# Values of key blocks 1 to 3 in one run of TensorE work, and the value projection two batch rows ahead

## The chip, the cores and the metric

One NeuronCore of one Trainium2 chip runs the whole program. The metric is device time in microseconds (us) of one launch, from three runs. TensorE is called PE in the profile (PEld is its weight load), VectorE DVE, ScalarE ACT, GpSimd POOL, and SyncE SP, which only issues DMAs here.

## The reference

The input is 8 batch rows of 512 tokens with 128 channels. Three stages of work alternate with mixture-of-experts layers:

- a first attention, 16 heads of 8 channels, whose keys and values are halved in length by a convolution (512 queries against 256 keys, no mask);
- a second attention, causal, 512 against 512, with its own layer norm;
- a third and a fourth attention, causal, run together as one stage of 16 batch rows.

Per head, `att = softmax(q k^T / sqrt(8))` (masked above the diagonal where it is causal) and `out = att v`, followed by an output projection and a residual sum.

## The kernel before

`attention` (L511) works in units. A unit is one batch row b and one group g of 4 heads, so a batch row has 4 units (u = 4b + g), and a causal stage has 32 or 64 units. In each causal unit PE goes through 12 slots. Slot i computes a score chunk of unit u (L781, keys on the partitions, then mask matmuls L648) and a "max" tile of unit u+2 (L665, queries on the partitions, then mask matmuls L648). ACT exponentiates each chunk out of PSUM into `pt` (L858), and DVE reduces each max tile to `mx` (L1008). Score chunks rotate over `RING = 3` PSUM banks and max tiles over three others, so slot i may start only when ACT has read chunk i-3 and DVE has read tile i-3 (`score_wait`, `max_wait`, `before`). Slots 0 to 3 are 512 columns wide, 4 to 7 are 384, 8 and 9 are two heads of 256, and 10 and 11 two heads of 128.

Everything else that PE does is put between slots by `order(u)`: for each name the dictionary `when` gives the slot behind which it stands. Each engine's program is written out from the same order, so a copy on ACT or DVE stands at the same place in its queue.

- `value_p` and `value0`, `value1` are the matmuls of `pt` with the values (`values`, L725). For one key block kb they are 8 instructions, 32 columns of the array each, four side by side. `early` says which key blocks are done in the unit itself, and `late` which are done in the next unit under the name `value_p`.
- `max_T` is a transpose of `mx` (L680). Its result goes by ACT (`nm`, L890), four POOL operations (L1161 to L1167) and three DMAs (L1290, `put_max`) into row 52 and the next two of `qa`. Slot 0 of the next unit waits for their landing (`m_landed`).
- `o_T`, `ctx_T`, `out` (L737, L744, L751) transpose and project the attention's result. `x_T`, `q`, `k`, `v` (L689, L695, L702, L707) prepare a later batch row. All of these, and `max_T`, use PSUM bank `MISC` one after another (`take_misc`), and each is copied out by ACT (x_T, q, k, ctx_T, nm) or DVE (o_T, out, v).
- `value_rows` (L998) copies v from PSUM to the buffer `vst`, and `spread` on POOL (L1150) takes it from there to `vs`, one group of heads a unit.
- `f_moments`, `f_T`, `f_l` prepare the next mixture layer's routing; `moments` are layer-norm moments for batch rows to come (L149, L152).

Of the kernel before, what the change touches and what calls it, by code (L numbers as in the profile page):

```python
# [25 lines left out]
P = 128  # L26
# [7 lines left out]
B, S, C = 8, 512, 128  # L34
T = B * S
NT = T // P
TB = S // P
H, D = 16, 8
# [472 lines left out]
def attention(nc, k, segments, r):  # L511
# [17 lines left out]
    LATE_ROOT = {3: 3, 7: 4, 11: 5}  # L529
    LAST = len(r.phases) - 1  # L530
    SENT_IN = {-6: (0, 1), -5: (1, 4), -4: (4, 5), -3: (5, 8), -2: (8, 12), -1: (12, 16)}
    entered = lambda b: sum(first <= b for first, n in ENTRY_GROUPS)

    if causal:
        chunks = ([(0, (h,), 512) for h in (0, 1, 2, 3)] + [(1, (h,), 384) for h in (0, 1, 2, 3)]
                  + [(kb, heads, S - kb * P) for kb in (2, 3) for heads in ((0, 2), (1, 3))])
        maxes = ([(3, (h,), 512) for h in (1, 0, 3, 2)] + [(2, (h,), 384) for h in (1, 0, 3, 2)]
                 + [(qb, heads, (qb + 1) * P) for qb in (1, 0) for heads in ((1, 3), (0, 2))])
        when = {"value_p": 2, "max_T": 2, "o_out": 2, "nm": 2, "o_T": 5, "value0": 8, "x_T": 8, "k": 5, "ctx_T": 8,
                "q": 11, "v": 11, "out": 5, "value1": 11, "moments": 4, "f_moments": 4, "f_T": 8, "f_l": 11,  # L540
                "late0": 0, "late2": 6, "late_root": 0, "choose": 6, "ranks": 5, "mark": 6, "f_rows": 0,
                "choose0": 8, "ranks0": 8, "find0": 9, "choose1": 7, "choose2": 9, "choose3": 1, "ranks1": 9,
                "find1": 10, "choose4": 1}
        last_front = (11, 8, 11, 3, 8, 11)
        early, late = ((0,), (1,)), (2, 3)
    else:
        chunks = [(kb, (h,), 512) for kb in range(KB) for h in (0, 1, 2, 3)]
        maxes = [(qb, heads, nk) for qb in range(TB) for heads in ((1, 3), (0, 2))]
        when = {"value_p": 2, "max_T": 2, "o_out": 2, "nm": 2, "o_T": 4, "x_T": 5, "k": 5, "ctx_T": 5, "value0": 6,
                "q": 7, "v": 7, "out": 7, "moments": 3, "f_moments": 3, "f_T": 5, "f_l": 7,  # L550
                "late0": 0, "late2": 4, "late_root": 0, "choose": 5, "ranks": 4, "mark": 5, "f_rows": 0}
        last_front = (7, 5, 7, 3, 6, 7)
        early, late = ((0,),), (1,)
# [10 lines left out]
    def order(u):  # L564
# [6 lines left out]
            events += [("o_out", u // 2 - 1), ("o_T", u // 2 - 1)]  # L571
        if u + 1 < U:
            events += [("max_T", u + 1), ("nm", u + 1)]
        if g == 0 and b + 1 < NB:
            events += [("v", b + 1)]
        if u in LATE_ENTRY:
            events += [("late0", LATE_ENTRY[u])]
        if u - 1 in LATE_ENTRY and u:
# [7 lines left out]
        if u == U - 2:  # L586
            events += [("f_rows", b - 1)]
        if g == 3 and FIRST + 3 <= b < NB - 1:
            events += [("f_T", b - 3), ("f_l", b - 3)]
        fronts = []  # L590
        if b == NB - 1 and g < 3:
            names = (("f_T", 4),), (("f_l", 4), ("f_T", 5)), (("f_l", 5), ("f_T", 6), ("f_l", 6))
# [41 lines left out]
    with nc.Block() as block:  # L634
# [3 lines left out]
        def _(pe):  # L638
# [168 lines left out]
            for t in range(NMX):  # L807
                max_tile(1, t)
                if t in (2, 5):
                    project(ENTRY[t // 3], 1)  # L810
            project("k", 1)
            for u in range(U):
                for name, n in order(u):
                    if name == "score":
                        slot(u, n)
                    elif name == "max_T":
                        max_transpose(n)
                    elif name == "value_p":
                        for kb in late:
                            values(n, kb)  # L820
                    elif name[:-1] == "value":
                        for kb in early[int(name[-1])]:
                            values(n, kb)
                    elif name in ("x_T", "q", "k", "v"):
                        project(name, n)
                    elif name in ("o_T", "ctx_T", "out", "f_T", "f_l"):
                        tail(name, n)
                    elif name in ("ranks0", "ranks1"):
                        take_misc()
                        ranks(pe, k, r, n)  # L830
                        misc[0] = (s.ranks_read, n + 1)
                    elif name == "ranks":
                        ranks(pe, k, r, n)
# [91 lines left out]
        def _(dve):  # L925
# [67 lines left out]

            def value_rows(b):
                dve.wait_ge(*s.v_full.at(b + 1))
                if b >= 1:
                    dve.wait_ge(*s.vs_ready.at(4 * b))
                nc.vector.tensor_copy(k.vst[:, 0:KB, :], PS[:, MISC, 0:KB * P].rearrange("p (t c) -> p t c", c=P))\  # L998
                    .then_inc(s.v_free.h, 1)

            def max_tile(u, t):
# [52 lines left out]
            for t in range(NMX):  # L1054
                max_tile(1, t)
                if t == 5 and conv:
                    convolve(1)
            entry(2, 2)
            entry_deviations(2)
            for u in range(U):  # L1060
                for name, n in order(u):
# [6 lines left out]
                    elif name in ("o_T", "out"):  # L1068
                        tail(name, n)
                    elif name == "late2":  # L1070
                        entry(2, n)
                    elif name == "late_root":
                        entry_deviations(n)
                    elif name == "moments":
                        later_moments(n)
                    elif name == "f_moments":
                        front_moments(n).then_inc(s.fm_ready.h, 1)
                    elif name == "f_rows":
                        front(n)
                    elif name == "choose0":  # L1080
                        if n == 0:
                            dve.wait_ge(*s.gl_free.at(r.phases[0][1] // TB))
                        choose(nc, k, route, r, 0, (n,))
                    elif name in ("choose1", "choose2", "choose3"):
                        if n == 0:
                            dve.wait_ge(*s.gl_free.at(r.phases[1][1] // TB))
                        choose(nc, k, route, r, 1, (n,))
                    elif name in ("find0", "find1"):
                        find_ranks(nc, k, route, r, n)
                    elif name in ("choose", "choose4"):  # L1090
                        dve.wait_ge(*s.gl_free.at(r.phases[n][1] // TB))
                        choose(nc, k, route, r, n)
                    elif name == "mark":
                        find_ranks(nc, k, route, r, n)
                        dve.wait_ge(*s.pv_done.at(U - 1))
                        mark_tiles(nc, k, route, r, 0)
# [28 lines left out]
        def _(pool):  # L1125
# [18 lines left out]
            def spread(b, g):  # L1144
                if g == 0:
                    pool.wait_ge(*s.v_free.at(b + 1))
                if b >= 1:
                    pool.wait_ge(*s.pv_done.at(4 * b - 3 + g))
                pair, n = g // 2, g % 2
                pool.tensor_copy(k.vs[:, g, 0:KB, :, n * D:(n + 1) * D], k.vst[:, 0:KB, pair * 64:pair * 64 + 64]  # L1150
                                 .rearrange("p t (h n d) -> p t h n d", h=HG, n=2)[:, :, :, n, :]).then_inc(s.vs_ready.h, 1)

            def max_split(u):
# [510 lines left out]
def program(nc, a, out):  # L1664
    ctx = ExitStack()
    with ctx:
# [39 lines left out]
        k.work = sb("work", [4, S])  # L1706
        k.q32, k.k32, k.rest, k.restk = (k.work[:, i, :] for i in range(4))
        k.parts = sb("parts", [2, 3, S], BF16)
        k.vst = sb("vst", [TB, C])
        k.vs = sb("vs", [G, TB, HG, 32])  # L1710
        k.qa, k.ka = sb("qa", [2, G, 2, S], BF16), sb("ka", [2, G, 2, S], BF16)
        k.mx = sb("mx", [2, 16])
# [325 lines left out]
```

## Time and profile before

| | us |
|---|---|
| median of 3 runs | 1950.85 (1948.93 to 1954.16) |
| the profiled execution's own time | 1948.95 |
| its span in the trace | 1947.2 |
| PE busy | 1548.6 (80%) |
| DVE busy | 1297.8 (67%) |
| POOL busy | 1078.7 (55%) |
| ACT busy | 966.4 (50%) |

The span is the time from the first to the last instruction; 1.75 us of the execution lie around it. A row of the timeline gives an instruction's or a run's start, its length, engine, line, operation and what it writes and reads, and in brackets how long the engine sat idle before it and what released it. Of matmuls that overlap, the length of a run is that of their union.

### The profile page before, as it was taken

How to read it: one execution, taken by the hardware profiler on the slowest of the kernel's cores; microseconds unless marked ns; L12 is line 12 of the kernel's file. 1: busy time of each engine (PE TensorE's matmuls, PEld its weight loads, DVE VectorE, ACT ScalarE, POOL GpSimd, SP SyncE). 2: the span in 40 equal slices, each digit the busy share in tenths (PEclk: the TensorE clock that was granted, in tenths of full speed). 3: DMA queues.
4: the chain of work that ended last, by engine and by line, in shares of the span. 5: the costliest groups of instructions: out<-in, count | busy, mean ns of one | idle time of the engine just before them, and what ended most of it. 6: DMA issues, size and time to landing. Idle time of an engine off the chain costs nothing. (4 is left out here: it accounts for less than half of the span.)

```text
span 1947.2 us, 46256 instructions
## 1 busy us (share of the span) xinstructions
PE 1548.6 (80%) x17646; PEld 941.7 (48%) x17646; DVE 1297.8 (67%) x3322; ACT 966.4 (50%) x2039; POOL 1078.7 (55%) x1712
## 2 busy tenths in 40 slices
PE   5648788876599999854798599999999999744993
PEld 4532333345255555433576355555555555423772
DVE  7348888782688878734421688888888887544324
ACT  4215667732166677520233166777777776411331
POOL 3447766505378775545355376555757765552552
PEclk9977999977599999865799599999999999755996
DMA  8443322204333223100343442332323322001445
GB/s 288 112 131 104 90 82 80 75 23 123 114 120 104 82 88 99 42 28 23 114 138 98 138 126 84 92 100 78 113 84 98 97 81 83 26 23 56 141 130 156
DMA packets 233185, 188.08 MB, mean 97 GB/s; under 512 B 30044, under 2 KB 221368, under 8 KB 232326
## 3 DMA queue, kind: packets, MB, share of 16 engines
q1 hardware_dynamic: 222582, 166.36, 28.5%
q0 software_dynamic: 10240, 18.76, 2.9%
q8 instruction: 141, 2.31, 0.5%
q14 instruction: 78, 0.64, 0.1%
q10 hardware_dynamic: 144, 0.00, 0.0%
HBM read 104.34 MB, written 80.74 MB: 95 GB/s over the span
## 5 line engine op out<-in xcount | busy, mean ns | idle before, releaser
L1008 DVE TENSOR_REDUCE mx<-PS 128x2 f32<-128x512 f32 (+3 forms) x1408 | 784.2, 612 | 189.0 <-PE PS L648 137.5
L858 ACT ACTIVATE pt<-PS 128x512 f32<-128x512 f32 (+2 forms) x1408 | 667.6, 537 | 312.1 <-PE PS L648 227.6
L665 PE MATMUL PS<-ka,qa 52*128 52x256 bf16 (+3 forms) x2048 | 461.7, 305 | 65.2 <-DVE mx L1008 47.4
L781 PE MATMUL PS<-qa,ka 55*128 55x512 bf16 (+3 forms) x1792 | 459.7, 321 | 41.3 <-DMA qa<-nm 17.8
L725 PE MATMUL PS<-pt,vs 128*32 128x512 f32 (+3 forms) x3584 | 349.6, 481 | 2.3 <-issue 1.5
L648 PE MATMUL PS<-mask_q,identh 64*128 64x64 bf16 x3072 | 299.5, 193 | 1.5 <-issue 1.4
L648 PE MATMUL PS<-mask_k,identh 64*128 64x64 bf16 x3072 | 299.0, 192 | 0.9 <-issue 0.9
L781 PEld LDWEIGHTS PS<-qa,ka 55*128 55x128 bf16 x1792 | 166.9, 94 | 273.7 <-issue 119.3
L648 PEld LDWEIGHTS PS<-mask_k,identh 64*128 64x128 bf16 x3072 | 249.2, 97 | 51.7 <-issue 6.8
L648 PEld LDWEIGHTS PS<-mask_q,identh 64*128 64x128 bf16 x3072 | 252.4, 98 | 31.0 <-issue 8.9
L1161 POOL CAST nm<-nm 16x128 bf16<-16x128 f32 x128 | 36.2, 283 | 340.1 <-ACT nm L890 329.3
L665 PEld LDWEIGHTS PS<-ka,qa 52*128 52x128 bf16 x2048 | 172.1, 95 | 97.9 <-DVE mx L1008 63.3
L415 POOL DMA_INDIRECT xe_rows<-xn,slot x128 | 128.4, 1003 | 93.2 <-DVE slot L402 56.2
L1398 PE MATMUL PS<-pt 128*128 128x128 f32 x1280 | 155.7, 280 | 9.4 <-ACT pt L1422 6.3
L1422 ACT ACTIVATE pt<-PS,f1b 128x512 f32<-128x512 f32 x128 | 87.6, 687 | 152.2 <-PE PS L1386 148.9
L1386 PE MATMUL PS<-pt 128*128 128x512 f32 (+1 forms) x384 | 155.6, 551 | 4.5 <-issue 2.6
L1398 PEld LDWEIGHTS PS<-pt 128*128 128x128 f32 x1280 | 151.0, 196 | 11.8 <-issue 11.6
L1524 POOL DMA_INDIRECT y_rows<-pt,idx x80 | 79.4, 992 | 113.5 <-DVE pt L1489 95.2
L725 PEld LDWEIGHTS PS<-pt,vs 128*32 128x32 f32 x3584 | 82.2, 110 | 75.7 <-issue 27.3
L1386 PEld LDWEIGHTS PS<-pt 128*128 128x128 f32 x384 | 74.4, 204 | 58.8 <-issue 52.4
L1479 DVE TENSOR_SCALAR pt<-PS,l2w,l2b 128x512 f32<-128x512 f32 x32 | 25.9, 810 | 98.1 <-PE PS L1376 93.2
L1516 POOL DMA_INDIRECT pt<-xn_rows,idx x32 | 31.3, 977 | 98.1 <-issue 56.5
(249 smaller groups left out, 2333.4 us busy)
## 6 DMA issues: line engine op xcount, KB each, us to landing
pt<-in_f_w SPq DMA_DIRECT2D x96, 256.0 KB
qa<-q_parts SPq DMA_DIRECT2D x256, 96.0 KB, 2.3
ka<-k_parts SPq DMA_DIRECT2D x192, 96.0 KB, 2.3
q_parts<-parts SPq DMA_DIRECT2D x32, 384.0 KB, 3.4
k_parts<-parts SPq DMA_DIRECT2D x24, 384.0 KB, 2.6
xn<-y_rows SPq DMA_DIRECT2D x32, 256.0 KB, 3.2
hid<-y_rows SPq DMA_DIRECT2D x32, 256.0 KB, 3.7
q_parts<-parts SPq DMA_DIRECT2D x32, 256.0 KB, 3.2
```

The source lines that it names most:

```text
L415: pool.indirect_dma_start(k.xe_rows[:, :], bass.IndirectOffsetOnAxis(k.slot[:, c, t:t + 1], 0), k.xn[:, t * P:(t + 1) * P], None, bounds_c ...
L648: mm = pe.matmul(PS[:, bank, col + j * HALF:col + (j + 1) * HALF], k.identh[half * HALF:(half + 1) * HALF, j, :], table[half * HALF:(half ...
L665: mm = pe.matmul(PS[:, bank, i * n:(i + 1) * n], k.qa[rows, b % 2, g, h // 2, qb * P:(qb + 1) * P], k.ka[rows, b % 2, g, h // 2, 0:n], sta ...
L725: mm = pe.matmul(PS[32 * h:32 * h + 32, O_BANK, q0:S], k.vs[:, g, kb, h, :], k.pt[:, u % 2, at[c] + i * n:at[c] + (i + 1) * n], start=(kb ...
L781: mm = pe.matmul(PS[:, bank, i * n:(i + 1) * n], k.ka[rows, b % 2, g, h // 2, kb * P:(kb + 1) * P], k.qa[rows, b % 2, g, h // 2, q0:S], st ...
L858: nc.scalar.activation(k.pt[:, u % 2, at[c]:at[c] + len(heads) * n], PS[:, SC_BANK + c % RING, 0:len(heads) * n], ACT.Exp, scale=SCORE_SCA ...
L1008: nc.vector.tensor_reduce(out, PS[:, MX_BANK + t % RING, 0:len(heads) * n] .rearrange("p (h n) -> p h n", n=n), AX.X, ALU.max).then_inc(s. ...
L1161: pool.tensor_copy(hi, full).then_inc(s.nm_hi.h, 1)
L1386: pe.matmul(PS[:, H_BANK + f, 0:capacity], k.w1[:, par, f * P:(f + 1) * P], k.xeT[:, par, 0:capacity], start=True, stop=True).then_inc(s.h ...
L1398: mm = pe.matmul(PS[:, Y_BANK + par, t * P:(t + 1) * P], k.hT[:, par, f, t * P:(t + 1) * P], k.w2[:, par, f, :], start=(f == 0 and t == 0) ...
L1422: nc.scalar.activation(k.hT[:, e % 2, f, 0:capacity], PS[:, H_BANK + f, 0:capacity], GELU, bias=w.b1[:, e * FC + f:e * FC + f + 1]).then_i ...
L1524: pool.indirect_dma_start(k.y_rows[:, :], bass.IndirectOffsetOnAxis(k.idx[:, 1, n:n + 1], 0), k.ys[e % RING_E][:, t, :], None).then_inc(s. ...
```

## The change

In the causal stages the four places between slots (behind 2, 5, 8 and 11) become three (behind 3, 7 and 11), with `value_p` now holding key blocks 1, 2 and 3 in place of 2 and 3, and key block 0 behind slot 7. `x_T` and `ctx_T` move from behind slot 8 to behind slot 11, `q` stays there. The value projection `v` of batch row b+1, done in group 0 of b, becomes that of b+2, done in group 3 of b; so a second buffer for its rows is needed (`vst_other`, which lies over the convolution's `cv`; in the first attention the two halves of `vst` serve), and v of row 1 is done before the first unit. In the first attention `k`, `f_T`, `f_l` and `v` move too. `f_l` now stands in group 0 of the following batch row. DVE gets a wait for its own end behind `f_moments`.

```diff
+    vst = lambda b: (k.vst, k.vst_other)[b % 2] if causal else k.vst[:, b % 2 * KB:(b % 2 + 1) * KB, :]
     if causal:
-        when = {"value_p": 2, "max_T": 2, "o_out": 2, "nm": 2, "o_T": 5, "value0": 8, "x_T": 8, "k": 5, "ctx_T": 8,
-                "q": 11, "v": 11, "out": 5, "value1": 11, "moments": 4, "f_moments": 4, "f_T": 8, "f_l": 11,
+        when = {"value_p": 3, "max_T": 3, "o_out": 3, "nm": 3, "o_T": 7, "value0": 7, "x_T": 11, "k": 7, "ctx_T": 11,
+                "q": 11, "v": 11, "out": 7, "moments": 4, "f_moments": 4, "f_T": 9, "f_l": 5,
...
-        last_front = (11, 8, 11, 3, 8, 11)
-        early, late = ((0,), (1,)), (2, 3)
+        last_front = (9, 8, 11, 5, 9, 11)
+        early, late = ((0,),), (1, 2, 3)
     else:
-        when = {"value_p": 2, "max_T": 2, "o_out": 2, "nm": 2, "o_T": 4, "x_T": 5, "k": 5, "ctx_T": 5, "value0": 6,
-                "q": 7, "v": 7, "out": 7, "moments": 3, "f_moments": 3, "f_T": 5, "f_l": 7,
+        when = {"value_p": 2, "max_T": 2, "o_out": 2, "nm": 2, "o_T": 4, "x_T": 5, "k": 4, "ctx_T": 5, "value0": 6,
+                "q": 7, "v": 7, "out": 7, "moments": 3, "f_moments": 3, "f_T": 6, "f_l": 3,
...
-        if g == 0 and b + 1 < NB:
-            events += [("v", b + 1)]
+        if g == 3 and b + 2 < NB:
+            events += [("v", b + 2)]
...
         if g == 3 and FIRST + 3 <= b < NB - 1:
-            events += [("f_T", b - 3), ("f_l", b - 3)]
+            events += [("f_T", b - 3)]
+        if g == 0 and FIRST + 4 <= b:
+            events += [("f_l", b - 4)]
...
             project("k", 1)
+            project("v", 1)
...
             def value_rows(b):
                 dve.wait_ge(*s.v_full.at(b + 1))
-                if b >= 1:
-                    dve.wait_ge(*s.vs_ready.at(4 * b))
-                nc.vector.tensor_copy(k.vst[:, 0:KB, :], ...
+                if b >= 2:
+                    dve.wait_ge(*s.vs_ready.at(4 * (b - 1)))
+                nc.vector.tensor_copy(vst(b)[:, 0:KB, :], ...
...
+            value_rows(1)
             entry(2, 2)
...
                         front_moments(n).then_inc(s.fm_ready.h, 1)
+                        dve.wait_ge(*s.fm_ready.at(n - FIRST + 1))
...
-        k.vst = sb("vst", [TB, C])
+        k.vst, k.vst_other = sb("vst", [TB, C]), k.cv[:, :, :].rearrange("p j (t c) -> p (j t) c", c=C)
```

## Rows read from the trace of the kernel before

**Rows 1.** Busy time by window: stretch, its length, engines' busy time, PEclk, DMA share, GB/s.
```profile
155.20:410.00 254.80, 213.36 (x1582) 89.62 (x1581) 215.82 (x469) 170.96 (x341) 162.10 (x317) 0.95 0.28 84
1115.20:1667.30 552.10, 524.17 (x8437) 305.13 (x8436) 464.65 (x1037) 396.91 (x889) 352.35 (x638) 0.99 0.31 93
```

**Rows 2.** The same view for single units: four of one batch row, then a fifth.
```profile
1331.29:1340.61 9.32, 9.02 (x150) 5.70 (x146) 8.00 (x16) 6.54 (x15) 8.81 (x14) 1.00 0.45 153
1340.61:1348.71 8.10, 8.10 (x145) 4.94 (x142) 6.75 (x14) 6.37 (x14) 4.86 (x9) 1.00 0.40 110
1348.71:1357.29 8.58, 8.58 (x139) 4.76 (x135) 7.24 (x15) 6.52 (x15) 1.63 (x5) 1.00 0.19 52
1357.29:1365.92 8.63, 7.81 (x135) 4.05 (x132) 7.40 (x20) 6.40 (x15) 5.73 (x10) 1.00 0.22 60
...
1124.23:1132.12 7.89, 7.69 (x137) 4.45 (x134) 6.16 (x13) 6.30 (x14) 7.24 (x12) 1.00 0.35 93
```

**Rows 3.** Timeline of PE in the unit at 1340.61: its four pieces.
```profile
1341.55 0.86 PE L725 MATMUL PS<-pt,vs 128*32 128x256 f32 x16
1342.34 0.28 PE L680 MATMUL PS<-ident,mx 128*16 128x128 f32 x1
...
1343.41 1.16 PE L751 MATMUL PS<-a1wo,ctxT 128*128 128x128 f32 x8
...
1345.45 0.63 PE L689 MATMUL PS<-ident,xa 128*128 128x128 f32 x4
1346.00 1.07 PE L725 MATMUL PS<-pt,vs 128*32 128x512 f32 x8
...
1347.81 0.19 PE L648 MATMUL PS<-mask_q,identh 64*128 64x64 bf16 x1
1347.93 0.85 PE L725 MATMUL PS<-pt,vs 128*32 128x384 f32 x8
```

**Rows 4.** Timeline of PE, the pieces that only other units of the row have.
```profile
1336.25 0.63 PE L744 MATMUL PS<-ident,ctx 128*128 128x128 f32 x4 [0.30 <-DVE ctx L1020]
...
1338.73 1.16 PE L707 MATMUL PS<-a1wv,xnT 128*128 128x128 f32 x8
...
1351.52 0.66 PE L737 MATMUL PS<-ident,osb 128*128 128x128 f32 x4
...
1355.45 1.13 PE L695 MATMUL PS<-xnT,afwq 128*128 128x512 f32 x2
```

**Rows 5.** Groups by shape, 1331.29 to 1365.92: count, then busy us, mean ns, idle before.
```profile
L1008 DVE TENSOR_REDUCE mx<-PS 128x1 f32<-128x512 f32 x16 | 10.3, 686 | 2.8 <-PE PS L648 2.6
L1008 DVE TENSOR_REDUCE mx<-PS 128x1 f32<-128x384 f32 x16 | 8.1, 549 | 0.0
```

**Rows 6.** Timeline of DVE in the unit at 1340.61, then of ACT around 1357.29.
```profile
1341.14 3.56 DVE L1008 TENSOR_REDUCE mx<-PS 128x1 f32<-128x512 f32 x6 [0.52 <-PE PS L648]
...
1356.62 0.69 ACT L880 ACTIVATE work<-PS,afqb 128x512 f32<-128x512 f32 x1 [0.61 <-PE PS L695]
1357.78 1.58 ACT L858 ACTIVATE pt<-PS 128x512 f32<-128x512 f32 x3 [0.47 <-PE PS L648]
```

**Rows 7.** Timeline of PE, slots 3 to 8 of the unit at 1124.23.
```profile
1126.17 0.39 PE L781 MATMUL PS<-qa,ka 55*128 55x512 bf16 x1
...
...
1127.31 0.33 PE L781 MATMUL PS<-qa,ka 55*128 55x384 bf16 x1 [0.20 <-ACT pt L858]
1127.46 0.33 PE L665 MATMUL PS<-ka,qa 52*128 52x384 bf16 x1
...
1128.15 0.27 PE L781 MATMUL PS<-qa,ka 55*128 55x256 bf16 x1
```

**Rows 8.** Timeline, the three DMAs of `put_max` in two units, and one wait for them.
```profile
221.69 1.59 SPq L1290 DMA_DIRECT2D qa<-nm  x3
...
224.40 0.39 PE L781 MATMUL PS<-qa,ka 55*128 55x512 bf16 x1 [1.63 <-DMA qa<-nm]
...
1344.64 1.59 SPq L1290 DMA_DIRECT2D qa<-nm  x3
```

More of the change, by code:

```diff
@@ L995, in value_rows @@
                 dve.wait_ge(*s.v_full.at(b + 1))
-                if b >= 1:
-                    dve.wait_ge(*s.vs_ready.at(4 * b))
-                nc.vector.tensor_copy(k.vst[:, 0:KB, :], PS[:, MISC, 0:KB * P].rearrange("p (t c) -> p t c", c=P))\
+                if b >= 2:
+                    dve.wait_ge(*s.vs_ready.at(4 * (b - 1)))
+                nc.vector.tensor_copy(vst(b)[:, 0:KB, :], PS[:, MISC, 0:KB * P].rearrange("p (t c) -> p t c", c=P))\
                     .then_inc(s.v_free.h, 1)
@@ L1149, in spread @@
                 pair, n = g // 2, g % 2
-                pool.tensor_copy(k.vs[:, g, 0:KB, :, n * D:(n + 1) * D], k.vst[:, 0:KB, pair * 64:pair * 64 + 64]
+                pool.tensor_copy(k.vs[:, g, 0:KB, :, n * D:(n + 1) * D], vst(b)[:, 0:KB, pair * 64:pair * 64 + 64]
                                  .rearrange("p t (h n d) -> p t h n d", h=HG, n=2)[:, :, :, n, :]).then_inc(s.vs_ready.h, 1)
```

## The prediction

> **What bounds the kernel now.** I read the busy time by window first, because the share over the whole span mixes stages. In the long causal stage PE is busy 524 of 552 us at a granted clock of 0.99 [rows 1]; DVE has 465 and ACT 397. The first attention is another case: PE 213 of 255 us, DVE 216, neither full [rows 1]. Then I took single units. Three of the four units of a batch row have PE busy for all or nearly all of 9.32, 8.10 and 8.58 us; the fourth idles 0.8 us of 8.63 (it holds the DVE work `moments`) [rows 2]. A row takes 34.63 us. So PE's order of work sets the pace there, and DVE (6.75 to 8.00 us a unit) is close behind. That second fact matters, since PE and DVE can only overlap by as much as three PSUM banks hold.
>
> The timeline of PE shows what a unit is made of: slots, which run without a gap, and four pieces between them. A piece costs its own busy time and 0.05 us: from the last mask at 1347.81 to the next unit's start at 1348.71 are 0.90 us, for 0.85 of values [rows 2, 3].
>
> **The pieces now.** With that 0.05, in us: values 2 and 3 with `max_T` 0.86 + 0.28, overlapping, 1.12; `out` 1.21; `o_T` 0.71; `q`, and `k` of the same shape, 1.17; key block 0 alone 1.12, key block 1 alone 0.90; `x_T` (the shape of `ctx_T`, 0.63) and block 0 1.72; `ctx_T` and block 0 with a wait of 0.30 for DVE 2.04; `v` and block 1 1.99; `q` and block 1 1.96 [rows 3, 4]. The units of a row have pieces of 5.86, 4.95, 4.91 and 4.31, together 20.0. The second unit (8.10) has no idle time, so its twelve slots take 8.10 - 4.95 = 3.15, four times that is 12.6, and 34.63 - 12.6 - 20.0 = 2.0 us a row are waits between slots.
>
> **What the change saves.** How much of a piece is the break itself? Block 0 has 128 columns more than block 1 and takes 1.07 against 0.85, so 0.22 for 128 columns; 384 columns are then 0.66, and 0.24 of the 0.90 is the break [rows 3]. A row has 16 breaks now and 12 after: 4 x 0.24 = 0.96. The wait of `ctx_T` goes too, 0.30: `o_T` will stand behind slot 7 and `ctx_T` behind 11, and slot 11 can't start before DVE has read tile 8, which it does behind `o_T`'s division. Pieces after: 20.0 - 1.26 = 18.7 us a row. Moving `v` by one unit moves 1.16 us of PE [rows 4] and a DVE copy of 512 columns, 0.7 by the reduce of the same width [rows 5], and adds neither.
>
> **What it costs.** Now each piece comes after three slots, and three banks are what may be filled ahead. After it comes a fourth slot, whose bank DVE must have emptied. A unit starts at 1340.61 and DVE starts on tile 0 at 1341.14, 0.53 later [rows 2, 6]; the reduce takes 0.69 [rows 5]; to PE's next start I add 0.06, so that it is 1.28 (the 1.29 measured below has this distance in it). Three slots take 0.84, from 1340.61 to just before the values at 1341.55 less a lead of 0.12 [rows 2, 3]. Wait: 0.43. A slot of 384 columns is by estimate 0.05 shorter than the 0.28 of one of 512, and its tile there as much sooner: 0.48 + 0.55 + 0.06 = 1.09 against 0.70, wait 0.39. For slots 8 to 11 (the first two hold 512 columns again, the last 256) I take 0.41, the mean.
>
> The trace has one place with the same situation. The unit at 1124.23 has no piece behind slot 5. Its slot 3 starts at 1126.17, and slot 6 should start three slots, 0.28 + 0.23 + 0.23 = 0.74, later. Its score starts at 1127.31, released by ACT, and its max tile at 1127.46, 1.29 after slot 3: 0.55 late [rows 7]. And this unit, which lacks the `out` piece of 1.21 us, is only 0.21 shorter than the second one (7.89 against 8.10) [rows 2]. The breaks behind every third slot are time in which DVE and ACT catch up; PE pays for it anyway.
>
> There is one more loss. A copy on ACT stands in front of the next exponentials. Now every such piece but `out` and `o_T` has values behind it that hide the copy (`x_T`, `ctx_T`, `q`), and `k`'s falls between slots 5 and 6. After, `x_T`, `ctx_T` and `q` stand alone behind slot 11. The copy of q begins 0.11 after its matmuls end and takes 0.69, so the exponential of slot 0 starts at 0.80 instead of 0.49 (1357.78 - 1357.29) [rows 2, 6]. An exponential takes 0.60 (three, half a microsecond apart, end 1.58 after the first's start), so slot 3 waits until 0.80 + 0.60 + 0.06 = 1.46 instead of 0.84: 0.61 in place of 0.43. `v`'s copy on DVE does the same. The copy `o_out` in every second unit comes just before slot 4's exponential, but begins while PE still transposes; I add 0.09 there, 0.48 for 0.39.
>
> Waits after, for a row: slot 3 4 x 0.61 = 2.44, slot 7 2 x 0.39 + 2 x 0.48 = 1.74, slot 11 4 x 0.41 = 1.64: 5.8. The row's sum: 12.6 + 18.7 + 5.8 = 37.1 against 34.6. DVE's `moments` no longer count: they stand behind slot 4, and the tiles they delay are wanted only behind the piece after slot 7. That is inside the sum, since the 2.0 of old waits isn't carried over. So +2.5 us a batch row.
>
> The Trainium skill speaks against the change as well: Perfetto Trace Analysis, section Identifying Performance Opportunities, says that the same gap again and again on the engine that should be saturated can mean that SBUF or PSUM has no room for the next tile. By that rule PE would show one gap for each group of four slots; the trace so far agrees with it in the one unit above, with 0.55 us. The sum would be the same by it.
>
> **The sum.** There are 24 causal batch rows. The last of each stage is full of other waits, and I leave both out. Of the 22 left the six at b = 0 to 2 have late layer-norm work on DVE, and waits there that a break would have cost nothing; half the loss for them. 16 x 2.5 + 6 x 1.25 = 48. `v` of row 1 stands ahead of each causal stage, where PE comes from idling: its 1.16 us doubled if the clock is at its lower level there, and 1.16 given back in unit 0, so 1 a stage, 2 for both. Where the `f_` pieces stand alone they break a group of four, which gives back what their break costs; nothing. The first attention: PE and DVE both have 40 us to spare in 255, v and k move into unit 3 of a row; nothing, at most 3 us either way. DVE's added wait: 12 times some 0.1, beside other idle time.
>
> 1948.95 (span 1947.2 and 1.75 around it) + 48 + 2 = 1999 for an execution like the profiled one, whose time is 1.9 under the median of the runs. I take **2001 us**.
>
> **Bounds.** Below: if ACT's copies cost nothing, and only 0.43 + 0.39 + 0.41 of waits a unit stay, a row has 4.9 of waits, +1.6, and the sum is 1951 + 16 x 1.6 + 6 x 0.8 + 2 = 1983; with a break worth 0.1 more, 4 x 0.1 x 22 = 9 less, 1974. Above: the full loss in all 22 rows, 55, and waits of the measured 0.55 at slots 7 and 11 and 0.61 at slot 3, 6.8 a row in place of 5.8, another 22: 2030.
>
> **Rivals.**
>
> *The path of the maxima ends last.* `max_T` moves behind slot 3 and all of the values. It starts at 1.73 in a unit now; then at 1.46 + 0.28 + 0.12 + 0.66 (block 1) + 0.79 (blocks 2 and 3, 1341.55 to 1342.34) = 3.3. The DMAs start 2.30 after it (1344.64 - 1342.34) [rows 3, 8] and have landed 2.7 after their start, as where PE waited for them (221.69 to 224.40) [rows 8]: 8.3, in a unit of 9.3 on average: 1 us of slack, where the second unit now has 8.1 - 1.73 - 2.3 - 2.7 = 1.4. For: POOL and SP have other work queued ahead of it in the first and last unit of a row, and each may make it later. It decides from 1 us on. If it then ends last in every unit by half a microsecond, 22 x 2 = 44 more: 2045. 0.08.
>
> *PE gains.* The waits at the fourth slots lie under what PE's queue does meanwhile, or the banks are free sooner than I read. Then what counts is pieces and slots: 22 x 1.26 = 28 less, 1923, and if half the old waits go too, 1900. It decides at 1.26 us of new waits a row, so 0.1 at each of 12 fourth slots. For: 0.24 a break is real. Against: 0.55 was measured in one such slot [rows 7]. 0.08. The Trainium skill, same page, section Optimizing Tensor Performance, says that matmul groups should rotate through PSUM banks so that the reading of one overlaps the matmuls of the next. Both versions do rotate, and by this rule the reading is covered, which is this rival's 1923.
>
> *It cancels.* New waits of 12 x 0.27 = 3.3 us a row, beside no old ones: within 0.3% of before. Against: 0.27 is less than the reduce's 0.69 allows. 0.04.
>
> *The clock falls* in the causal stages, as PE idles more. The first attention has PE busy at 84% and a granted clock of 0.95 [rows 1]; the sum gives the causal ones about 31.3 of 37.1, 84% too. Going from 0.99 to 0.95 over the 552 us of the long stage and about half as much of the short one is 0.04 x 830 = 33, most of it hidden behind the new waits; a third of it, 11, gives 2012, inside the range. It is part of the chance of the main case, 0.80.
>
> So faster by over 0.3% 0.08, within 0.3% 0.04, slower by over 0.3% 0.88; 0.3% is about what a measurement of this kernel tells from no change. The range, 1968 to 2035, takes in the bounds of the main case and a few us for the start, the first attention and the clock on either side.
>
> **What would show it.** In the profile after: a causal unit of 9.0 to 9.6 us instead of 8.1 to 9.3; PE idle before L781 or L665 at slots 3, 7 and 11 with ACT `pt` L858 and DVE `mx` L1008 as releasers, some 0.4 to 0.7 each; 12 pieces in a row, of 18.7 us; the wait of `ctx_T` gone, `moments` without a wait. DVE and ACT idle in front of a unit's first tile for longer, about 1 us. The prediction fails if slot 3 doesn't wait, if the waits of `qa<-nm` come to tens of us, or if the row at 1331 to 1366 is under 34.6.

## The result, and the profile after

The changed kernel took 2028.26 us (median of 4 runs, 2021.62 to 2040.24), the kernel before in the same measurement 1950.67: a ratio of 1.040, 95% interval 1.035 to 1.044. The forecast was 2001 with a range to 2035, so the sign and the size came, 27 us short of the median. The profiled execution took 2026.74, its span is 2025.0 against 1947.2.

Where did 77.8 us go? The first view is the busy time by window, cut at the first score of each attention stage and at its end. Of the kernel before (stretch, length, busy PE, PEld, DVE, ACT, POOL, granted clock, DMA):

```profile
155.20:409.70 254.50, 213.06 (x1581) 89.52 (x1580) 215.56 (x467) 170.86 (x341) 162.10 (x317) 0.95 0.28 84
409.70:537.88 128.18, 76.02 (x516) 57.24 (x513) 72.88 (x264) 24.08 (x50) 47.84 (x54) 0.65 0.33 97
537.88:877.92 340.04, 295.50 (x4358) 170.19 (x4359) 256.07 (x628) 210.87 (x467) 221.70 (x370) 0.92 0.26 79
877.92:1115.16 237.24, 171.13 (x1028) 121.84 (x1024) 95.15 (x282) 54.47 (x83) 112.75 (x118) 0.77 0.34 101
1115.16:1725.73 610.57, 560.13 (x8773) 325.48 (x8774) 490.20 (x1117) 416.18 (x931) 377.40 (x668) 0.96 0.28 87
```

The same view of the changed kernel, and below it the four units of one steady batch row, which answer to [rows 2]:

```profile
155.91:415.47 259.56, 217.85 (x1577) 88.55 (x1577) 215.28 (x467) 170.46 (x340) 159.89 (x315) 0.94 0.27 81
415.47:546.72 131.25, 78.88 (x525) 59.72 (x521) 71.67 (x254) 25.09 (x51) 47.72 (x54) 0.65 0.35 102
546.72:908.45 361.73, 305.29 (x4351) 177.50 (x4351) 257.30 (x629) 210.64 (x467) 220.74 (x370) 0.90 0.23 72
908.45:1150.82 242.37, 170.61 (x1029) 122.35 (x1030) 94.77 (x281) 55.02 (x84) 112.39 (x118) 0.76 0.34 103
1150.82:1802.84 652.02, 580.81 (x8767) 339.83 (x8767) 492.79 (x1121) 413.82 (x931) 375.93 (x668) 0.94 0.26 80
...
1303.54:1312.30 8.76, 8.30 (x138) 4.89 (x138) 7.40 (x15) 5.93 (x14) 7.61 (x13) 1.00 0.33 111
1312.30:1321.45 9.15, 8.61 (x143) 5.41 (x142) 7.09 (x14) 6.18 (x14) 3.33 (x7) 1.00 0.49 149
1321.45:1330.51 9.06, 8.49 (x136) 4.65 (x136) 7.36 (x15) 6.42 (x15) 1.62 (x5) 1.00 0.13 36
1330.51:1340.13 9.62, 9.08 (x141) 5.28 (x140) 7.64 (x20) 6.87 (x15) 5.31 (x10) 1.00 0.17 44
```

The causal stages are 21.7 and 41.4 us longer, the stretches ahead of them 3.1 and 5.1, the first attention 5.1. A steady row takes 36.59 instead of 34.63, with the same DVE and ACT work in it: PE now idles in all four units, 0.46 to 0.57 us by this view, where two units had none.

The timeline shows where. Here is PE from slot 3 on in the unit at 1330.51, then DVE and ACT from the unit's start:

```profile
1331.84 0.39 PE L784 MATMUL PS<-qa,ka 55*128 55x512 bf16 x1 [0.32 <-ACT pt L862]
...
1332.23 1.50 PE L728 MATMUL PS<-pt,vs 128*32 128x384 f32 x24
1333.66 0.28 PE L683 MATMUL PS<-ident,mx 128*16 128x128 f32 x1
1333.87 0.33 PE L784 MATMUL PS<-qa,ka 55*128 55x384 bf16 x1
...
1331.05 1.29 DVE L1012 TENSOR_REDUCE mx<-PS 128x1 f32<-128x512 f32 x2 [0.72 <-PE PS L651]
...
1330.62 0.69 ACT L884 ACTIVATE work<-PS,a1qb 128x512 f32<-128x512 f32 x1 [0.66 <-PE PS L698]
1331.20 2.05 ACT L862 ACTIVATE pt<-PS 128x512 f32<-128x512 f32 x4
```

Line numbers are three or four higher than before. The copy of q ends at 1331.31, 0.80 into the unit. The exponentials behind it start at 1331.20 and follow each other half a microsecond apart, each 0.60 long, so the bank that slot 3 needs is read at about 1331.80. Slot 3 starts 1.33 into the unit instead of 0.84: 0.49 late, of which the trace books 0.32 as idle, released by ACT. From slot 3's score to slot 4's are 2.03 us; less 0.27 for the slot itself, the piece between them (24 matmuls of values in one run, and `max_T`) takes 1.76, as the sum had it (1.12 and 0.90 less a break of 0.24 is 1.78). So both steps are in this one place: the break was saved, and a wait of twice its size came.

A slot's max tile can start later than its score, because it has another reader. These are the score and the max tile of slot 3, then of slot 11, in the unit at 1303.54:

```profile
1304.68 0.39 PE L784 MATMUL PS<-qa,ka 55*128 55x512 bf16 x1
...
1305.00 0.39 PE L668 MATMUL PS<-ka,qa 52*128 52x512 bf16 x1
...
1311.23 0.23 PE L784 MATMUL PS<-qa,ka 55*128 55x128 bf16 x1
...
1311.38 0.23 PE L668 MATMUL PS<-ka,qa 52*128 52x128 bf16 x1
```

Slot 3's score comes 0.57 after slot 2's, where a slot takes 0.27: ACT holds it 0.30. DVE holds the max tile 0.31 more, and in slot 11 another 0.14. Over the twelve fourth slots of this row, from the starts in the timeline, the scores are 4.1 us late together (slot 3 0.30 to 0.50, slot 7 0.28 to 0.40, slot 11 0.27) and the max tiles 1.1 beyond that, in seven of the twelve.

PE's waits in the long causal stage, before and then after (us in total, times, longest):

```profile
PE PS L665 <- DVE mx L1008: 22.0, 27, 1.7
PE PS L781 <- issue: 10.0, 4, 4.9
PE PS L744 <- DVE ctx L1020: 4.2, 14, 0.3
...
PE PS L781 <- ACT pt L858: 1.1, 4, 0.4
```

```profile
PE PS L784 <- ACT pt L862: 31.5, 69, 9.4
PE PS L668 <- DVE mx L1012: 13.5, 17, 2.0
...
PE PS L784 <- DMA qa<-nm: 2.3, 1, 2.3
```

What PE waits for has changed hands: ACT 31.5 in place of 1.1, DVE 13.5 in place of 22.0, and the wait of `ctx_T` is gone. These idle times are a lower bound of the loss, since overlapping matmuls hide the first part of a late start.

### The profile page after: what moved, and what is told of

It reads as the page before. It is cut to its first block and busy times, and to the rows that moved or that the text cites. A ratio compares the mean times of both kernels' runs of the same rounds, so it can differ in the third digit from the quotient of the medians.

```text
span 2025.0 us, 46271 instructions
## 1 busy us (share of the span) xinstructions
PE 1583.9 (78%) x17646; PEld 963.6 (48%) x17646; DVE 1300.1 (64%) x3322; ACT 965.4 (48%) x2039; POOL 1074.6 (53%) x1712
## 5 line engine op out<-in xcount | busy, mean ns | idle before, releaser
L784 PE MATMUL PS<-qa,ka 55*128 55x512 bf16 (+3 forms) x1792 | 475.7, 325 | 92.2 <-ACT pt L862 40.6
L668 PE MATMUL PS<-ka,qa 52*128 52x256 bf16 (+3 forms) x2048 | 473.8, 309 | 56.6 <-DVE mx L1012 38.1
L728 PE MATMUL PS<-pt,vs 128*32 128x512 f32 (+3 forms) x3584 | 338.7, 491 | 1.0 <-ACT pt L862 0.7
L651 PE MATMUL PS<-mask_q,identh 64*128 64x64 bf16 x3072 | 305.9, 194 | 0.0
L651 PE MATMUL PS<-mask_k,identh 64*128 64x64 bf16 x3072 | 304.0, 192 | 0.0
L651 PEld LDWEIGHTS PS<-mask_k,identh 64*128 64x128 bf16 x3072 | 253.8, 97 | 53.3 <-issue 9.4
L728 PEld LDWEIGHTS PS<-pt,vs 128*32 128x32 f32 x3584 | 94.2, 113 | 112.0 <-issue 63.8
```

What stands on the lines that cost most here:

```text
L651: mm = pe.matmul(PS[:, bank, col + j * HALF:col + (j + 1) * HALF], k.identh[half * HALF:(half + 1) * HALF, j, :], table[half * HALF:(half ...
L668: mm = pe.matmul(PS[:, bank, i * n:(i + 1) * n], k.qa[rows, b % 2, g, h // 2, qb * P:(qb + 1) * P], k.ka[rows, b % 2, g, h // 2, 0:n], sta ...
L728: mm = pe.matmul(PS[32 * h:32 * h + 32, O_BANK, q0:S], k.vs[:, g, kb, h, :], k.pt[:, u % 2, at[c] + i * n:at[c] + (i + 1) * n], start=(kb ...
L784: mm = pe.matmul(PS[:, bank, i * n:(i + 1) * n], k.ka[rows, b % 2, g, h // 2, kb * P:(kb + 1) * P], k.qa[rows, b % 2, g, h // 2, q0:S], st ...
```

## The experiments

Times are medians, with the ratio to the kernel before in the same measurement (1951.6 for the first four kernels, 1951.4 for the next three) and its 95% interval. "Row" is a steady batch row of the long causal stage, read from the windows.

**Three slots, with the rest of the change.** From the changed kernel:

```diff
-        when = {"value_p": 3, "max_T": 3, "o_out": 3, "nm": 3, "o_T": 7, "value0": 7, "x_T": 11, "k": 7, "ctx_T": 11,
-                "q": 11, "v": 11, "out": 7, ... "f_T": 9, "f_l": 5,
+        when = {"value_p": 2, "max_T": 2, "o_out": 2, "nm": 2, "o_T": 5, "value0": 8, "x_T": 11, "k": 5, "ctx_T": 11,
+                "q": 11, "v": 11, "out": 5, ... "f_T": 8, "f_l": 8,
```

> All parts of the change but the places in the causal stages: the values of blocks 1 to 3 stay one run and v stays two rows ahead, but the pieces stand behind slots 2, 5, 8 and 11 again. If the wait for a PSUM bank at each fourth slot is the cause, a row has 12.6 us of slots, 7.0 + 3.8 + 4.5 + 3.8 = 19.1 of pieces and under 2 of waits, 33.4 in place of 34.6 before and 36.6 after: 22 rows give 26 less than before, the start of the stages and the first attention some 11 more, so about 1935 us (1925 to 1947). If the long run of values or the earlier v is the cause, at least half of the 78 us stays: 1990 or more.

Measured 1968.41 (1965.39 to 1971.89), ratio 1.009 [1.008, 1.011]. The spacing, with the places of `f_T` and `f_l` that were set back with it, is worth 60 us of the 78. The size missed: 33 us above the forecast of 1935, though a row is 0.7 less than before (33.4 expected):

```profile
1309.56:1343.48 33.92, 33.07 (x554) 19.86 (x553) 29.18 (x62) 25.71 (x58) 20.98 (x47) 1.00 0.33 100
```

So something that I had priced at 2 us cost far more, outside the steady rows. v was the suspect, and a kernel below takes it alone.

**Places alone**, the four-slot spacing without the merged run: block 1 back as `value1` behind slot 11 (`early, late = ((0,), (1,)), (2, 3)` in the changed kernel).

> The change, but block 1 of the values is a run of its own again, now behind slot 11; pieces stand behind slots 3, 7 and 11. If the distance of four slots is the cause, the loss stays: the pieces of a row are 0.6 longer than in the change, and the ACT copies behind slot 11 are hidden again by the values, which gives back some 0.3 a row: 2020 to 2045 us. If one long run of values is the cause, the time falls back to 1950 to 1975.

2019.83 (2016.39 to 2020.76), 1.035 [1.033, 1.036], at the lower edge of the forecast; the row is 36.84. The spacing does it whether the values are merged or not.

**Block 0 behind slot 11** (`"value0": 11` in the changed kernel).

> The change with the values of block 0 behind slot 11, after x_T, ctx_T, q and v, instead of behind slot 7. Pieces and their sum stay the same; what changes is that the ACT copies of x_T, ctx_T and q run under the values and no longer delay the exponential of slot 0. Theory: slot 3 then waits for DVE alone, 0.43 in place of 0.50 to 0.59, and the copy of k delays slot 8: 0.1 to 0.3 a row, 2015 to 2027 us. If the copies are the main part of the waits, more than 1 us a row comes back: under 2005.

2052.69 (2048.91 to 2058.23), 1.052 [1.050, 1.055], and a row of 37.85: a miss in sign, 24 us slower than the changed kernel. Slot 3's score did behave: its distance from the start is 1.14 us in each of the four units, where the changed kernel has up to 1.33. But the piece behind slot 7 was now short in two units (0.92 from slot 7 to slot 8, against 1.92), and there the max tile of slot 11 came 0.59 after its score, where the changed kernel has 0.15. In the fourth unit slots 8 and 9 took 0.76 and 0.46 in place of 0.36 and 0.33. My reading, which no run isolates: what a wait costs depends on the length of the piece too, and time that a piece has beyond the readers' backlog is lost to them.

**v alone**, from the kernel before: v of b+2 in group 3, its second buffer, v of row 1 ahead; the places and the values as before.

> The kernel before, with only v moved: v of row b+2 in group 3 with the second row buffer, v of row 1 ahead of the units. Places, values, f_l and the first attention's other places as before. Theory: each causal stage starts 2.8 us later (0.78 of waiting for the copy of k and 2.08 of matmuls at the lower clock) and gets 1 back in unit 0; the rows themselves stay at 34.6: 1950 + 4 to 8, 1956 us. If v's place is the cause of much of the loss, 1975 or more.

1966.90 (1965.43 to 1967.80), 1.008 [1.006, 1.010]: 15 us, where I gave it 4 to 8. The row is unchanged (34.63). Much of the cost sits at the starts. In the changed kernel and in this one v of row 1 waits for the copy of k and then runs at a granted clock of 0.50, the lower level; this is the changed kernel:

```profile
1145.96 2.07 PE L705 MATMUL PS<-xnT,a1wk 128*128 128x512 f32 x2
1148.81 2.08 PE L710 MATMUL PS<-a1wv,xnT 128*128 128x128 f32 x8 [0.78 <-ACT work L889]
```

2.86 us on the path, against 1.16 in [rows 4]. With v alone the two starts were 3.5 and 3.7 us later, and nothing came back in unit 0: it took 11.97 us where the kernel before had 9.07, though v of row 1 is gone from it. The kernel with v alone, then the kernel before, and below them DVE and PE with v alone:

```profile
1130.98:1142.95 11.97, 10.36 (x114) 5.57 (x113) 9.58 (x29) 6.11 (x13) 8.02 (x12) 0.54 0.27 87
1115.16:1124.23 9.07, 9.07 (x122) 5.30 (x122) 8.09 (x21) 6.51 (x14) 5.83 (x10) 0.87 0.54 186
...
1131.09 0.69 DVE L1000 COPY cv<-PS 128x512 f32<-128x512 f32 x1 [4.30 <-PE PS L708]
...
1135.34 0.61 PE L666 MATMUL PS<-ka,qa 52*128 52x512 bf16 x1 [1.61 <-DVE mx L1010]
```

In DVE's program `value_rows(1)` now stands ahead of a layer-norm entry and of the first max tiles of unit 2. So DVE idles 4.30 us for v, and PE idles 0.78 before v and 1.61 before the fourth max tile. By windows of 1 us the granted clock stays at 0.50 until 1142, 11 us into the unit; in the kernel before PE had no idle time there, and the clock stood at 1.00 from 3 us into the unit on. The first rows of the causal stages became 2.0 and 4.0 us longer.

This kernel also has a cost that the changed one hasn't. In rows with `f_` pieces v now stands in one piece with `f_l`, and the two share the bank `MISC`: in one such unit slot 11's start and the next unit's are 4.12 us apart against 2.12 before, for 1.16 of v. Four of the six late causal rows are 0.9 to 2.0 longer, the other two 1.1 and 1.7 shorter. The first attention is 5.0 longer, 3.6 of it in rows 3 to 7: there v and `f_l` share the last piece of group 3, and in two of the rows it takes 2.60 from the last slot to the next unit, against 1.70 and 1.31 before.

**Three breaks fewer at the old spacing**, from the kernel before:

```diff
-        when = {... "x_T": 8, ...
+        when = {... "x_T": 11, ...
...
-        events += [(f"value{i}", u) for i in range(len(early))]
+        events += [(f"value{i}", u) for i in range(len(early)) if i == 0 or g == 3]
...
-                        for kb in late:
+                        for kb in ((1,) if causal and n % G < 3 else ()) + late:
```

> The kernel before with one part of the change alone, at the spacing of before: in groups 0 to 2 of a batch row block 1 joins blocks 2 and 3 in one run (group 3 keeps it behind slot 11, so that no place is empty), x_T behind slot 11 for that. v, its buffer and all other places are those of before. My theory (a break costs 0.24 us, a piece after every third slot costs no wait): three breaks fewer a row, 0.72, less what the copies of x_T, v and q take back now that they stand alone behind slot 11; the version with three slots, v moved and four breaks fewer had 0.72 less a row. So 0.4 to 0.7 a row, 22 rows: 9 to 15 less, 1936 to 1943. Rival 1 (the break is worth nothing, and what the three-slot version gained in its steady rows came from elsewhere): 1949 to 1954. Rival 2 (block 1 behind the next unit's slot 2 delays the values' accumulator or the copies' banks): over 1955.

1950.47 (12 runs, 1947.06 to 1954.47) against 1951.38 (17 runs), ratio 0.9994 [0.998, 1.000]: no difference, where I expected 9 to 15 us less. The row did shrink:

```profile
1294.87:1329.04 34.17, 33.02 (x556) 19.62 (x553) 29.28 (x63) 25.65 (x58) 20.93 (x46) 1.00 0.32 99
```

0.46 us a row, as forecast, and 1.1 in most of the first rows, 8.3 in all over the 22 rows. But the last rows of the two stages became 3.6 and 3.5 longer, why is open, and in each stage one row with routing work on DVE became 1.15 longer: at the start of two of its units the max tile of slot 0 came 1.4 us after its score, against 0.6 before. The piece behind slot 11 is shorter there by block 1, and DVE's work isn't.

**Maxima first**: `max_T` and `nm` ahead of the values and of `o_out` behind slot 3, in the changed kernel.

> The changed kernel with max_T and its copy ahead of the values and of o_out behind slot 3 in the causal stages, so that the path of the maxima starts some 1.4 us sooner. My theory (the waits come from four slots on three banks, the path of the maxima ends last in few units; its waits in the trace sum to 7.5 us against 2.5 before): 2018 to 2028, at most 10 less. The rival (the path of the maxima ends last): 40 us or more less, under 1990.

2041.37 (2037.22 to 2048.33), 1.047 [1.044, 1.049]. The rival falls: starting the path of the maxima 1.4 us sooner wins nothing, the row is 36.72. My own number missed too, by 13 us, and 7.4 of it lie where the order was not changed: the first attention took 266.93 against 259.56, at a granted clock of 0.91 against 0.94. The last row of the second attention took 83.7 against 73.5.

```profile
156.59:423.52 266.93, 226.00 (x1578) 90.19 (x1577) 215.35 (x467) 171.41 (x340) 160.31 (x315) 0.91 0.26 79
```

Why four executions of this kernel all stayed above 2037 is open.

**Places of the first attention** (`"k": 5`, `"f_T": 5`, `"f_l": 7` in the changed kernel's other branch).

> The changed kernel with k, f_T and f_l of the first attention back behind slots 5, 5 and 7; v stays as changed, and so do the causal stages. The first attention lasted 5.1 us longer in the changed kernel, and so it did in the kernel with v's move alone, whose k, f_T and f_l had the places of before. My theory (it is v that costs there, in group 3, where k, moments and v now meet): 0 to 3 us less, 2025 to 2029. The rival (the other places cost it): 5 less, 2021 to 2024, and the first attention back at 255.

2022.35 (2021.90 to 2027.05), 1.037 [1.035, 1.039]. The rival was right about rows 3 to 7 of that stage: 5.3 us longer in the changed kernel, they were 0.5 longer here, with v moved as before. So the places cost it, and v only where it shares a piece with `f_l`, as in the kernel with v alone. The stage itself didn't come back to 255: it took 258.82, because row 0 was 3.7 longer at a granted clock of 0.74 instead of 0.81.

**Shorter readers.** The last four kernels change the length of the work that empties the banks, and leave PE's work as it is. The first pair leaves out the maxima of half of the keys, in the changed kernel and in the kernel before:

```diff
 nc.vector.tensor_reduce(out, PS[:, MX_BANK + t % RING, 0:len(heads) * n]
-                        .rearrange("p (h n) -> p h n", n=n), AX.X, ALU.max) ...
+                        .rearrange("p (h n) -> p h n", n=n)[:, :, 0:n // 2 if causal else n], AX.X, ALU.max) ...
```

The second pair also leaves out half of each exponential, so that half of `pt` keeps old values:

```diff
+                wide = len(heads) * n // (2 if causal and u >= 2 else 1)
-                nc.scalar.activation(k.pt[:, u % 2, at[c]:at[c] + len(heads) * n],
-                                     PS[:, SC_BANK + c % RING, 0:len(heads) * n], ACT.Exp,
+                nc.scalar.activation(k.pt[:, u % 2, at[c]:at[c] + wide],
+                                     PS[:, SC_BANK + c % RING, 0:wide], ACT.Exp,
...
```

> The changed kernel with DVE's reduce of each causal max tile over half of its columns (the maxima of the other half of the keys are left out); PE, ACT and all places as they are. Estimate: a reduce of 512 columns falls from 0.69 to about 0.4 us. My theory (at the fourth slot either of two readers must have emptied the bank, and ACT's exponential, which starts behind the copies, is nearly as late as DVE's reduce: at slot 3 it is 0.31 to 0.61 late by my sum against DVE's 0.43): only what DVE adds beyond ACT goes, 10 to 30 us less, 1998 to 2018. Rival 1 (DVE alone sets the waits): 50 or more less, under 1980. Rival 2 (PE loses the time by itself, with no reader late): under 5 less.

> The same halved reduces in the kernel before, as the control. My theory (2.0 us of waits a row, of them DVE's moments, which stay): 5 to 20 less, 1930 to 1946, less than in the changed kernel. The rival (both kernels feel DVE alike, and the spacing does not matter to it): the same loss or gain as in the changed kernel.

> The changed kernel with both readers of the banks made short: the reduces over half of the columns, and from the third causal unit on each exponential over half of its chunk (the other half keeps old values). My theory: with both readers in time the waits at the fourth slots nearly vanish, and only slot 3 behind a copy of x_T, ctx_T or q still waits some 0.2 to 0.4. A row falls from 36.6 to 32 to 33.5, the kernel to 1935 to 1965. The rival (PE needs the time whoever reads): above 2000.

> The same two cuts in the kernel before. My theory: 2.0 us a row are all that waits can give back, less the moments: 20 to 40 less, 1910 to 1930; so the distance of the two kernels, 77 us whole, falls to 10 to 40, of which 15 is what moving v cost. The rival (spacing costs PE by itself): the distance stays above 60.

These four ran on a chip on which the kernel before itself took 1867.36 us, so only ratios to it and steady rows are compared; the changed kernel with whole readers wasn't run there. In the order above: 1896.07, ratio 1.016 [1.013, 1.018]; 1812.51, 0.972 [0.969, 0.974]; 1876.76, 1.005 [1.003, 1.007]; 1815.57, 0.971 [0.969, 0.973]. The steady rows, one line from each kernel's windows, in that order:

```profile
1225.29:1260.79 35.50, 33.48 (x554) 19.41 (x553) 20.01 (x62) 25.39 (x58) 17.86 (x33) 1.00 0.28 89
```

```profile
1180.52:1213.49 32.97, 32.79 (x556) 18.58 (x553) 19.16 (x62) 25.43 (x58) 17.87 (x33) 1.00 0.31 95
```

```profile
1225.06:1259.25 34.19, 33.56 (x553) 20.19 (x552) 19.61 (x62) 18.50 (x58) 17.89 (x34) 1.00 0.30 93
```

```profile
1184.88:1217.75 32.87, 32.59 (x557) 18.45 (x553) 19.17 (x62) 18.20 (x58) 17.89 (x33) 1.00 0.31 96
```

Take from each row 12.6 of slots and its pieces (18.6 in the changed order; 20.0 in the old one, of which 0.3 is the wait of `ctx_T`, gone with shorter reduces), and the waits are left:

| us a row | old order | changed order |
|---|---|---|
| as they are | 2.0 | 5.4 |
| DVE halved | 0.7 | 4.3 |
| DVE and ACT halved | 0.6 | 3.0 |

In the old order the waits are DVE's, and most go when DVE is shorter; a shorter ACT adds 0.1. In the changed order DVE alone gives back 1.1. That is just what the max tiles were later than the scores: with half reduces each max tile of a fourth slot starts within 0.05 us of its score, and the scores' 4.1 become 4.0. So ACT holds the rest, and both rivals of that pair fall. That neither cut removes the waits fits the lengths: an exponential of half the width still takes 385 ns where a whole one takes 602,

```profile
L863 ACT ACTIVATE pt<-PS 128x256 f32<-128x256 f32 x24 | 8.2, 385 | 7.8 <-PE PS L651 7.7
```

```profile
L862 ACT ACTIVATE pt<-PS 128x512 f32<-128x512 f32 x24 | 12.6, 602 | 6.6 <-PE PS L651 6.6
```

and a reduce 419 for 686, while PE starts a slot each 0.28 us. No reader tried here keeps pace within a group. My expectations of the time missed in three of the four, and in the fourth the row did: 34.19 where I expected 32 to 33.5. By the ratios, which for the whole readers come from other chips, the changed order gained 2.4% from shorter reduces, some 46 us for 10 to 30, and 3.5% from both, as expected; the old order gained 2.9%, 55 us, where I had said 5 to 20 and 20 to 40 (its steady row 1.66, the first rows of a stage 3 to 4 each). The distance of the two orders, 77 us as they are, is 84 with DVE halved and 61 with both, not 10 to 40.

**The kernel before once more**, for a second profile.

> The kernel before once more, unchanged, for a second profile of it: how far do the same rows of one kernel move from one execution to another? My theory: the steady rows at 34.63 to within 0.02, as in all kernels whose causal order is the same; the first attention (254.5 us) and the last row of a causal stage (74.1 and 73.3), where PE idles and the granted clock moves, differ by up to 3 us, so that the 5.1 us of the first attention in the changed kernel are only partly the change's. The rival: the first attention comes back within 0.5 us, and all 5.1 are the change's.

1950.46 (one run). Causal rows 3 to 11 of the long stage came back within 0.02 us, rows 1 to 7 of the first attention within 0.24, rows 3 to 7 within 0.04. Row 0 of the first attention moved by 1.4, the late rows of the causal stages by up to 1.2, one early row by 1.6. So the rival is wrong on the whole stage (1.5 us longer by itself), and my theory on its rows: the 5.3 us of rows 3 to 7 are the change's. Single late rows of other kernels move more: rows with the same causal order took 41.61 and 45.12 us in two of them.

## Why the prediction came out as it did

**Slots and pieces.** Right to the rounding. 12 pieces a row: 4 x 1.76 (values and `max_T`), 2 x 1.70 (`o_T` and block 0), 2.20 (`out`), 2.17 (`k`), 0.71, 0.71, 1.17 and 1.21 (`ctx_T`, `x_T`, `q`, `v`), together 18.6 against 18.7 predicted. The wait of `ctx_T` went. The break of 0.24 is real: in the kernel with three slots slot 3 comes 2.02 after slot 2, with all three blocks in the piece, and the two pieces that this one replaces took 1.37 and 0.90, so 0.25 is saved. With four breaks and the wait of `ctx_T` saved at the old spacing the row is 0.71 shorter; that the rest went to copies that lost their cover is my reading.

**Waits at the fourth slots.** Right in place and cause, a little large: 5.4 a row instead of 5.8. With the max tile counted, slot 3 is 0.61, 0.50, 0.44 and 0.50 late in the four units (0.61 predicted), slot 7 0.39 or 0.40 (0.39 and 0.48), slot 11 0.42 (0.41). So a steady row lost 1.95, not 2.5. The term that was too large is the copy on ACT ahead of slot 3. It does end 0.80 into the unit, as forecast (though by the rows it begins 0.04 after its matmuls end, not 0.11), but the next exponential starts 0.11 before that end. With block 0 behind slot 11, which covers the copies there, slot 3's score still waits 0.30: about 0.2 is the copy. The sum had DVE hold the fourth slots at 0.39 to 0.43 and ACT add only the copies. By the trace ACT is late in every one, by 0.27 or more even without a copy, and DVE is the later of the two in seven. That is why a shorter DVE gives back so little.

**The moments' wait** didn't carry over, as said: the row's fourth unit is 9.62, of which no DVE wait is booked.

**The sum.** The 22 rows gave 60.6 instead of 48. The ten rows between the early and the late ones gave 21.7 (25 predicted for them). The six early rows gave 12.8 instead of 7.5: halving their loss was wrong. The six rows with `f_` pieces and routing gave 26.1 instead of 15, 2.8 to 7.0 each. This is the mis-sized term: where the `f_` pieces stand alone I had costed them at nothing, because they break a group of four. Two rows of the six show how: DVE has routing work ahead of the first max tiles of two units, and those tiles start 1.4 us after their scores, against 0.6 before; the kernel with three merges alone has the same 1.4. In the others the cause is open. Part is the clock: in this kernel a row of the long stage had a stretch at 0.85 and took 44.37, while the kernel with the first attention's places restored has the same causal order and took 41.61. In the second attention it was the other way round (41.61 here, 45.12 there), so a few us of the 26 come and go without a change of the order.

```profile
1660.00:1683.50 23.50, 21.35 (x272) 11.51 (x267) 17.17 (x41) 13.23 (x29) 10.99 (x20) 0.85 0.12 33
```

**v ahead of each stage**: 8.2 us for the two starts instead of 2, of which 7.2 came with v alone. I had doubled its 1.16 rightly (2.08 at 0.50), but overlooked that it queues behind the copy of k (0.78) in the one PSUM bank. The 1.16 in unit 0 wasn't given back either: with v alone unit 0 took 2.9 longer in each causal stage, DVE late behind v and the clock at 0.50 for most of it. In the changed kernel the same unit took 2.1 longer.

**First attention**: +5.1 instead of 0 within 3. The 5.3 of rows 3 to 7 come from the places of `k`, `f_T` and `f_l`; which of the three is open. An engine with 40 us to spare over a stage can still be late at single pieces.

**The rivals.** The path of the maxima: PE's waits for `qa<-nm` in the causal stages sum to 7.5 us against 2.5 before, and an earlier `max_T` won nothing; it ends last in a unit of the steady rows only when both readers are halved (0.4 us in one of four). PE gains: the fourth slots are 0.4 to 0.6 us late in every unit, so the reading isn't covered there, while the three slots ahead start without a wait. The Trainium skill, Perfetto Trace Analysis, section Optimizing Tensor Performance, says to rotate matmul groups through PSUM banks so that their reading overlaps the next matmuls. The trace agrees for as many slots as there are banks, and not for the fourth. The Trainium skill, same page, section Identifying Performance Opportunities, says that a gap repeated on the engine that should be saturated can mean too little room for the next tile. The trace agrees, with twelve waits a row that sum to 5.4 us. The clock: 0.90 and 0.94 in the causal stages against 0.92 and 0.96, 0.02 and not 0.04. The prediction set its 84% of pieces and slots beside the first attention's 84% of busy time, which are two measures: a steady row is 94% busy by the profile (34.48 of 36.59 us), at a clock of 1.00.

No version tried beats the kernel before; the one with three breaks fewer equals it.

## What to carry to other kernels

When one engine feeds a ring of n banks, put its other work behind every n-th slot; a longer group saved a break (0.24 us here) and paid the readers' delay (0.4 to 0.6). That each piece should be as long as the slower reader is then behind is my reading of one kernel. Look at each reader's own tile: a wait that two readers share gives back only the difference when one of them is made shorter. Price a merge in the worst stretches as well: a saving of 0.46 us in each steady row was gone by the last row of each stage. Before moving a piece into a start-up, ask which bank and which copy it queues behind, what stands behind its copy on the other engine, and at which clock the start runs.

## What the runs showed of the hardware

- Readers of PSUM have a fixed part. From 512 to 256 columns ACT's exponential falls from 602 to 385 ns and DVE's reduce from 686 [rows 5] to 419, so by a straight line some 0.17 and 0.15 us stay.
- The same program differed by 4% between chips: the kernel before took 1867 us on one and 1951 on the others. In the four kernels profiled on the faster one the last row of a causal stage took 42 to 47 us instead of 72 to 84, while the unchanged rows of the first attention agree to 0.1 us (30.88 against 30.90 for a row). All four also have the shorter reduces, and the kernel before wasn't profiled there, so whether chip or edit makes the last row shorter isn't shown.
- A steady row is the same to 0.02 us in two profiles of one kernel. The rows that moved had another granted clock: 39.19 us at 0.96 and 37.64 at 1.00, 38.02 at 1.00 and 39.21 at 0.96, and row 0 of the first attention 34.40 at 0.81 and 35.76 at 0.75.
- A start can keep PE at the lower level for long. With PE busy without a gap ahead of and in unit 0 the granted clock rose from 0.50 to 1.00 within 3 us of the unit's start; with idle stretches of 0.78 and 1.61 us it stayed at 0.50 for 11 us, and the unit took 11.97 us instead of 9.07. It isn't the same each time: in the changed order with half reduces it was at 1.00 from 3 us on, back at 0.50 from 6 to 9 us, and at 1.00 again from 10.
